# Another hand-out order of 653 work items in an attention plus feed-forward kernel

## The reference, cut to what matters

```python
xn = _layernorm(x)
# attention: 8 heads, q and k have 3 numbers per head, v has 16
scores = einsum('bhtd,bhsd->bhts', q3, k3) * scale + q_on_dir[..., :, None] * k_on_dir[..., None, :]
scores = where(causal, scores, -inf)
attn   = softmax(scores, axis=-1)
att    = (attn @ v) @ Wo.T
# feed-forward: ternary weights times a scale per row, hidden width 512
h   = _bitlinear(xn, w_fc) + gate * (xn @ v.T @ fast_b.T @ u.T)
ffn = _bitlinear(relu(h) ** 2, w_proj)
out = x + att + ffn
```

## Time and profile before

| | us |
|---|---|
| median of three executions | 167.89 (167.42 to 167.95) |
| the profiled execution, its own time | 167.61 |
| its span, first to last instruction | 165.8 |
| TensorE matmul busy | 150.2 (91%) |
| VectorE busy | 127.1 (77%) |
| ScalarE busy | 124.1 (75%) |
| GpSimd busy | 70.7 (43%) |

### The profile page before, as it was taken

How to read it: one execution, slowest core, us unless ns; L and a number is a source line. 1 busy time by engine, 2 the same in 40 slices (tenths; PEclk the granted TensorE clock), 3 DMA queues, 4 the chain that set the end, 5 groups by cost and what they waited for, 6 DMA issues and landing times.

```text
span 165.8 us, 3297 instructions
## 1 busy us (share of the span) xinstructions
PE 150.2 (91%) x1105; PEld 64.2 (39%) x1109; DVE 127.1 (77%) x423; ACT 124.1 (75%) x222; POOL 70.7 (43%) x126
## 2 busy tenths in 40 slices
PE   6999899999999998999899989998499999869992
PEld 2464543523232423213132122234163255655682
DVE  5887899899999999999999979995386873111152
ACT  0888793589789879887899897887399989656700
POOL 4064029649777996157003830045016333411420
PEclk9999999999999999999999999999999999987998
DMA  3850000601042101501000100000202000210022
GB/s 94 202 177 0 6 2 2 124 0 32 4 86 44 32 0 30 101 0 31 4 0 0 34 4 2 0 4 0 63 0 54 14 0 0 62 37 2 0 67 65
DMA packets 16621, 5.71 MB, mean 34 GB/s; under 512 B 11292, under 2 KB 16476, under 8 KB 16604
## 3 DMA queue, kind: packets, MB, share of 16 engines
q1 hardware_dynamic: 16208, 5.34, 14.0%
q10 hardware_dynamic: 396, 0.16, 0.4%
HBM read 1.96 MB, written 1.05 MB: 18 GB/s over the span
## 4 chain that ended last, share of the span: by engine, by line
PE 50%; ACT 25%; DVE 7%; issue 7%; DMA 4%; SPq 3%; ACTq 1%; POOLq 0%; POOL 0%; DVEq 0%
ACT Pr L757 18%; PE obank L973 8%; PE vbank L791 8%; PE vbank L922 7%; PE abank L950 6%; PE abank L897 5%; PE abank L902 5%; DVE vbank L591 5%; ACT abank L743 4%; PE obank L798 3%; DMA QK<-X 3%; PE abank L878 3%; ACT r L737 2%; PE vbank L993 2%; DMA v_sb<-in_L_ffn_v 1%
## 5 line engine op out<-in xcount | busy, mean ns | idle before, releaser
L757 ACT ACTIVATE Pr<-abank 128x1024 f32<-128x1024 f32 (+3 forms) x96 | 74.8, 815 | 13.1 <-PE abank L950 7.1
L591 DVE CUSTOM_DVE_ANT_0 vbank<-vbank,mask_row 128x128 f32<-128x128 f32 (+3 forms) x128 | 59.0, 523 | 10.0 <-PE vbank L922 8.3
L922 PE MATMUL vbank<-QK 32*128 32x512 bf16 (+2 forms) x192 | 40.1, 328 | 1.0 <-DVE pm L591 0.7
L588 DVE TENSOR_REDUCE pm<-vbank 128x1 f32<-128x512 f32 x64 | 39.7, 682 | 1.5 <-PE vbank L922 0.9
L973 PE MATMUL obank<-Pr,V 128*32 128x512 f32 (+3 forms) x384 | 39.7, 498 | 0.1
L454 POOL TENSOR_SCALAR_AFFINE_SELECT Pr<-Pr 128x512 f32<-128x512 f32 x32 | 20.3, 638 | 40.4 <-ACT Pr L757 40.2
L950 PE MATMUL abank<-QK 32*128 32x512 bf16 (+3 forms) x192 | 30.1, 333 | 8.0 <-DMA QK<-X 5.1
L743 ACT ACTIVATE abank<-abank 128x256 f32<-128x256 f32 x64 | 23.7, 376 | 7.8 <-PE abank L950 7.4
L922 PEld LDWEIGHTS vbank<-QK 32*128 32x128 bf16 x192 | 11.7, 91 | 35.7 <-issue 16.6
L950 PEld LDWEIGHTS abank<-QK 32*128 32x128 bf16 x192 | 8.4, 91 | 31.1 <-ACT Pr L757 18.2
L791 PE MATMUL vbank<-w2T,r 128*128 128x128 f32 x128 | 18.6, 298 | 0.2 <-DVE pm L591 0.2
(11 more groups left out here) (111 smaller groups left out, 125.4 us busy)
## 6 DMA issues: line engine op xcount, KB each, us to landing
x_sb<-in_L_attn_x SPq DMA_DIRECT2D x4, 256.0 KB, 3.5
out_y<-xn SPq DMA_DIRECT2D x8, 128.0 KB, 1.9
wfc_sb<-in_L_ffn_w_fc SPq DMA_DIRECT2D x1, 256.0 KB, 3.6
wpj_sb<-in_L_ffn_w_proj SPq DMA_DIRECT2D x1, 256.0 KB, 2.8
QK<-X SPq DMA_TRANSPOSE x10, 2.4
k_sb<-in_consts SPq DMA_DIRECT2D x1, 64.0 KB, 2.8
Wv_sb<-in_L_attn_Wv ACTq DMA_DIRECT2D x1, 64.0 KB, 3.4
Wo_sb<-in_L_attn_Wo ACTq DMA_DIRECT2D x1, 64.0 KB, 3.8
```

The lines of the kernel that those rows point to most:

```text
L588: last = nc.vector.tensor_reduce(out=least, in_=s_n, op=ALU.min, axis=AX.X)
L591: last = nc.vector.tensor_tensor_reduce(out=s_n, in0=s_n, in1=mask_row[:, CH - keys:CH], scale=1.0, scalar=3.0e38, op0=ALU.add, op1=ALU.mi ...
L757: nc.scalar.activation(Pr[:, n % PSLOTS, 2 * pair:2 * pair + 2, 0:cols], src[:, :, 0:cols], ACT.Exp, scale=-1.0).then_inc(free(unit), 1)
L922: last = nc.tensor.matmul(o[:, at:at + keys], QK[r, quarter(b, chunk), 0, g, q0:q0 + P], QK[r, quarter(b, half), 1, g, 0:keys], start=True ...
```

## The change

Only `WEAVE` changes. No item is added, taken away or altered; the streams, their inner order, the waits and the shapes stay.

```diff
 WEAVE = """
-KKKKKKKKNKKWKKNCNNWKKXWFUQKNKKKIKKLNUKEVKFKKKNCKKMNMNEKKMMNUMMXKJKMMNMQHNMMVIMHMMXMMLHMMRHEMMQTVMMHMMHSAMOIKMG
-MMHRMMHMAMMSKSOGXMMKKAMOGMHMMAOGMHMMKMAAMDKOKGMMOAOKKSDMGKMAKTGAMOGMLDKMKMAOKGOGDAMMKSKAMODGMMOPMEAMGAOMPGMORJ
-DMAGAOOPGTPGDPMMAQMAMVPDMIMAMAMPLAMMJMAMMAPMAEnMPAMMHPnOMGAMOGHMMMPMAAMOMGOPAGMOMPGMAORDMMAOGPMGMAOSHDMGTAMDHM
-MMAADMMPAMMAMPAMMAMPPAPMMMAOPGAMOMMGAOPMnGDMAPOMGMRAOPDGAMOMMGAOSPGADMMOGTADMAPMAMPAMMAMPHPMMMAHPMMAAMPMAMMMOA
-GMPMOMAGPMAMMDOBGAOGYnRAOBOMGMGAOYGTAODPGAAMMDMPPDAMPMPMnABAMABAMYMAPAROMSMGAPMMAPOGMOMGDAOPMGDAOMPGAOTMMGMAPD
-OAGBOGMAOAYBOBMGGADPPDPROAGYAOGPABOGOAYDTGOAGOGBAOADOBGGBAOPDAPnPGAOGDOYDPBGAPPAOnGDOABYOGGYPDPBPnYBBYY
+KKNNKKKKWKKKKKNKWNKCKXWFUQKKNKILVKNFUECKENNKKKKMMUNKMKNNMMHMMHMMXMJXQMMMVMQHMNILMVHRMMHMMHMMETKMMSIMAOMHMGMHMK
+MAMKMKMOAGOKDMGAMKMROKGKAMMHMOMMGHMMKXMAOMSJKMAGKKMTAOMKGKMDOALGMKMOAMKKGOKMGAMKKMKAODMGORKGMMDAPMAMOPMDSMGODA
+GOAOPPTPMMGGAQAMVMPDDMMAAMPMMAPMInAMPMAMPHAMHMJMMAAEMOOMMGLPMMGEAMMOAPMOGMARPMMGOAGADMOOPGGAMOMGTAMHMMSHMMDAnM
+PMAAMMPMADDMPAPPMMAMAPMASMAOMMnGOGPMMAOMRPGMAAOMMODTPGGAMOMMAPGAOGOMGMAAMMDPDMDAMAMPPMAMMASMPHAMHMMPAMMAMnPAMO
+MGPMOGMAPMMMADPYOGROGTSAOBAGOMAGOBGAYOMGAAMMDPMDMAPMADMPPABAMMMABAYASOMGAOMPMMAPGnOAMMPGMAROPGMMOMAGDAOPOYTDGP
+GAOAMMOGBMDADGPPOAGOBAGOBRTADGYBPnOGDAOAOGBYAGOAYOGBDBAGAOOPGPPABYGAOGDOAODGPPDGBYDAAPPOPOGGnDPPnBBYBYY
 """
```

## The result

The changed kernel takes 159.69 us (159.39 to 160.00, 4 executions) where the kernel before took 167.92 (167.42 to 169.38, 4 executions) on the same chip: a ratio of 0.950, with a 95% interval of 0.944 to 0.956. The prediction said 162.3 us and a range from 160.6 to 165.5.

A forecast was written before the change was run, and what follows sets the result against it. VectorE, TensorE and ScalarE near full from 15.4 to 110.8 us, then TensorE, with two holes from late transposes. 167.61 − 2.9 − 2.2 − 1.2 + 0.3 + 0.4 = 162.0, median 0.28 above: 162.3 us, range 160.6 to 165.5.

The forecast's parts named there:

- first hole: TensorE's wait for the transpose before chunk 5's first `st`: maxT 5 ahead of y0a removes it whole, −2.9 us.
- second hole: TensorE's wait for the transpose before chunk 7's first `st`: maxT 7 ahead of y1a and y1b removes it, −2.2 us.
- clock: Half clock in chunk 7's sixteen `hid` matmuls goes once TensorE no longer stands before them: −1.2 us, bounds 0 and 1.2.
- opening and all other lists: Opening: an earlier rows copy on ScalarE delays VectorE's dense stream, +0.4 us, bounds −2 and +1.5; zero matmuls and GpSimd nothing.
- last items: Around pv 7.0 to 7.3 at the end: one more wait of pv for a mask, +0.3 us, bounds 0 and 1.2.
- only one hole closes: Rival, behind chunk 5: ScalarE's chain becomes the bound, gain about 2.2 us and the clock lost, 165.7 us; chance 0.10.
- it does not do what it says: Rival, at the transposes: something other than their place in the list, say DMA engines, held them, 167.9 us; chance 0.04.
- that case as a rival: Rival, dense stretch: it gains 2 us from VectorE's short idles instead of losing 0.4, 159.9 us; chance 0.08.
- clock term not gained: Rival, chunk 7: no clock fall in most runs of before, or one elsewhere after, 163.5 us; chance 0.17.
- Rows 1: Transpose for max 2.0, issued at 27.65 before: expected 1 to 2 us later, with 2.1 us in hand, costing nothing.
- the slower rival: Rival, rows 1: its transpose lands after TensorE reaches max 2.0; at 9 us late the kernel takes 169.2 us; chance 0.06.
- Zero matmuls: Four move from the opening into the dense stretch: 1.3 us of TensorE, covered by its 5.3 us idle, costing nothing.

The follow-up runs named there:

- both moves: Kernel before with only two items of SyncE's queue moved, maxT 5 ahead of y0a and maxT 7 ahead of y1a: 160.79 us, ratio 0.956.
- the filled holes: Kernel before with 13 zero matmuls added ahead of chunk 5's first `st` and 10 ahead of chunk 7's: 166.39 us, ratio 0.988.
- the mix: Order of the kernel before up to top 1, then the changed kernel's, with six fewer zero matmuls between top 1 and 52 us: 165.2 us, ratio 0.976.
- the mix at top 5: Order of the kernel before with maxT 5 moved, up to top 5, then the changed kernel's order: 161.29 us, ratio 0.955.

## Why the prediction was right and wrong

The sum in the prediction went from 167.61 to 162.0 for the profiled execution, 5.6 us. The profiled execution of the changed kernel took 160.0, 7.6 less. In the terms of the sum:

| term | forecast | measured | from |
|---|---|---|---|
| first hole | −2.9 | −3.05 | both moves, at chunk 5's first `st` |
| second hole | −2.2 | −2.27 | the same, at chunk 7's |
| clock | −1.2 | −1.55 | the same, at pv 7.0 |
| opening and all other lists | +0.4 | −0.61 (−1.29 from the first `qkv`) | new order against both moves, at chunk 5's first `st`: 114.55 against 115.16 |
| last items | +0.3 | −0.12 | the same two, from there to pv 7.3 (3.89 us less than before, against 3.77 with the moves alone) |
| sum | −5.6 | −7.55 | pv 7.3: 158.36 and 150.81 |
| median against the profiled execution | +0.28 | −0.3 | 159.69 against 160.0 |

Pv 7.3 comes at 150.81 instead of 158.36, 7.55 less; both moves alone give 6.82 of it there (6.87 at pv 7.0, where the clock's row is read), and 0.73 are left (0.61 + 0.12) for everything else.

The two profiled executions behind the −0.61 differ by 0.68 us at their first `qkv` (9.34 against 8.66), which fits the medians of the two kernels, 1.1 to 1.4 us apart where these two executions are 0.7.

**The holes.** Right by every row: transposes within 0.2 us of their prep, no wait for QK<-X, ScalarE not the next bound, chain at the end unchanged. The rivals *only one hole closes* and *it does not do what it says* are refuted.

**The opening and the lists: the step that failed, first.** "It can push VectorE's dense stream by up to 1.0 us ... Taken: +0.4." VectorE's stream is indeed late at top 0 (26.87 against 25.93), but top 1 is within 0.17 us again. Counted from the first `qkv` the new order is 0.3 us behind at top 0, 0.5 us ahead at top 1 and 0.25 us ahead at top 4 (81.55 against 81.80 us). The first `qkv` itself starts at 9.08 to 9.65 in five profiled kernels with the new opening and at 8.59 to 9.25 in eleven with the old one, 0.4 us later on average; so the opening does cost some tenths, and the lists behind it give them back before top 5. What I put at a loss, all lists but the queue's, is a gain: 0.6 us in this pair of executions, 1.3 from the first `qkv`, and some 0.9 when the later start of the new order is taken off again. I had that case as a rival (159.9 us, 0.08), gave it too little, and treated the 4.4 us of idle only as a cushion for losses. That its 159.9 lies next to the measured 159.69 is partly luck: it asks for 2 us in the dense stretch, and the clock and the offset of the median make up the rest. Between top 4 and top 5 the new order takes 1.0 us of VectorE's idle out, of which 0.4 count; it puts `ffn` and oT items of that stretch behind `max` items (the trace before has VectorE's waits of 0.41, 0.53 and 0.34 us there), but which of these moves does it was not tried one by one, and for the rest of the gain the cause stays open.

**The clock: the step that was mis-sized.** I priced one row, sixteen `hid` matmuls, 3.23 − 2.05. The window row beside it had TensorE dense for all of 3.40 us at 0.50, so the loss is up to 1.7, and 1.55 by the runs. Beyond that the term was taken for one execution only: most others of the kernel before lose more (2.5 us in the median by the filled holes), while all 16 executions of the changed kernel have a clock of 1.00. The rival *clock term not gained* was the wrong way about: the loss is met more often than the one trace shows, and it is gone with the holes. The offset of the median, +0.28 before and −0.3 after, was no part of the mechanism: the profiled execution of the changed kernel is the slowest of its four, all at 1.00, so this 0.6 us is scatter of the start, and luck.

**Last items.** No pv waited for a mask there: TensorE is busy 11.11 of 11.11 us. The +0.3 was a guess with both ends far apart, and its row was misread: the 0.6 us in two are waits of the weight loads (PEld), which overlap the matmuls, and no `pv` matmul of the kernel before waited for a mask by over 0.1 us. The one such wait of the changed kernel, 0.43 us at 109.87, lies ahead of chunk 5's first `st`.

**Rows 1.** Issued at 29.48, 1.8 us later than before, as forecast (1 to 2), and landed before its reader at 34.47: the slower rival needed a further 0.7 us to begin at all, and did not come.

**GpSimd.** Moving ternary 1, prep 1 and the squares cost nothing that shows: top 2 ends within 0.05 us of before.

**Zero matmuls.** "Cover enough: nothing" is right for the change as made, for a wrong reason: they are not covered load but hold up the clock. The four that the change moved out of the opening lie in the dense stretch now, 21 behind top 1 where there were 15. With six fewer there the mix lost about 1.5 to 2.4 us.

**Two sums.** The chances left outside the range add up to 0.28 (0.10, 0.08, 0.04 and 0.06), not "some 0.2"; and with prep 5 1 us later the transpose would land 0.2 to 0.9 us late, not 0.1 to 0.8. Neither changes the forecast.

## What to carry to other kernels

In an order that several engines follow, count the queue that issues DMAs as one of the engines: an item that is ready early and stands behind one that is ready late costs its whole wait, and two such swaps gave back 5.3 us of waiting here. A hole of 2 to 3 us in TensorE's work costs its length, and in most executions here a stretch of half clock behind one of the holes: price the whole stretch, not one row, and look at the clock of the other executions before taking the profiled one as typical. In a stretch of short idles of the bounding engine a searched order can gain, not only lose; but a gain there is worth only what the next engine lets through (0.46 of 1.00). And compare two profiled executions from the same early item on: here their starts differ by up to 0.7 us, half of what the last part of the change is worth.

## What the runs showed that was not expected

- The clock falls without a hole: TensorE was busy 2.82 of 4.00 us, no idle over 0.33 us, ahead of 7 us at half clock. In the mix at top 5 it fell at 97.2 us for 3.4 us after 3.56 of 4.20 us busy. The state table in Part 1 of the same page of the Trainium skill (TensorE: Matmul & The Clock Gate) has the clock fall after an idle window; further down, Part 1 tells of a kernel in which short idles between groups of matmuls made it go up and down. These stretches differ from the table and agree with the second: scattered idle was enough.
- What the first `qkv` is late by passes through. Ten profiled kernels with the old order up to top 1 and no fall of the clock there reach top 1 26.13 or 26.14 us behind their own first `qkv`, whether that starts at 8.59 or at 9.25.
- The 16 executions of the changed kernel spread from 159.19 to 160.09 us at the same clock of 1.00. That this is the spread in the opening is argued from four profiled executions with nearly its order (first `qkv` at 8.75 to 9.34, spans of 157.6 to 158.3 in the same order), not shown.
